# A four-layer vision network on one core: the first convolution and its channel sums, block-diagonal on the full array or as four 64x64 tiles

## What is computed

```python
x = x + _L0_conv_ref(_gn(x), ...)      # shifted-window attention
x = x + _L1_conv_ref(_gn(x), L1_conv_kernel, L1_conv_bias)
x = x + _L2_conv_ref(_gn(x), L2_conv_kernel)
x = x + _L3_conv_ref(_gn(x), ...)      # gated block

def _L1_conv_ref(x, kernel, bias):     # x is the normalised input
    xp = pad(x, one pixel)
    bin_k = sign(kernel)                                  # 3 x 3 x 64 x 64, +1 or -1
    alpha = mean(abs(kernel), axis=(0, 1, 2))
    bin_x = sign(xp)
    beta = mean(abs(xp), axis=3, keepdims=True)
    K = box_sum_3x3(beta) / 9
    return conv3x3(bin_x, bin_k) * (K * alpha) + bias
```

## Time and profile before

| | us |
|---|---|
| median of three runs | 238.65 |
| range of the three | 238.21 to 238.68 |
| profiled execution, its own time | 238.68 |
| its span, first to last instruction | 236.9 |

### The profile page before, as it was taken

How to read it: one execution, slowest core, us unless ns; L and a number is a source line. 1 busy time by engine, 2 the same in 40 slices (tenths; PEclk the granted TensorE clock), 3 DMA queues, 4 the chain that set the end, 5 groups by cost and what they waited for, 6 DMA issues and landing times.

```text
span 236.9 us, 6320 instructions
## 1 busy us (share of the span) xinstructions
PE 217.8 (92%) x2452; PEld 167.4 (71%) x2452; DVE 164.5 (69%) x379; ACT 138.3 (58%) x310; POOL 117.3 (50%) x119
## 2 busy tenths in 40 slices
PE   0668999999999999999999999978799999999995
PEld 0557999999999999999999897444355555434441
DVE  4337697967696968778766874789997865443633
ACT  2146587676767696866786555237654453395651
POOL 5147999995525679754699014837643311010000
PEclk9999999999999999999999999999999999999999
DMA  6997000000000000000000000001126730001012
GB/s 203 235 342 295 3 4 4 0 4 3 0 3 3 3 3 3 3 3 3 0 3 4 0 4 3 0 0 39 42 52 144 163 71 0 1 34 68 34 53 86
DMA packets 5453, 11.34 MB, mean 48 GB/s; under 512 B 816, under 2 KB 4016, under 8 KB 5296
## 3 DMA queue, kind: packets, MB, share of 16 engines
q1 hardware_dynamic: 5280, 10.68, 16.1%
q10 hardware_dynamic: 144, 0.26, 0.3%
HBM read 6.36 MB, written 1.61 MB: 34 GB/s over the span
## 4 chain that ended last, share of the span: by engine, by line
PE 80%; DVE 12%; issue 2%; DMA 2%; POOL 1%; ACT 1%; POOLq 0%; DVEq 0%; ACTq 0%
PE bank L653 18%; PE bank L664 12%; PE bank L681 11%; PE bank L881 5%; PE bank L628 5%; PE bank L882 4%; PE bank L783 4%; PE bank L906 3%; PE bank L896 3%; PE bank L640 3%; DVE x L1112 3%; DVE st L925 2%; PE bank L704 2%; PE bank L768 2%; DMA xw<-xw_in 2%
## 5 line engine op out<-in xcount | busy, mean ns | idle before, releaser
L202 POOL TENSOR_TENSOR kex<-ks,cst 64x784 f32<-64x784 f32 x31 | 47.3, 1525 | 20.7 <-issue 15.3
L986 DVE TENSOR_REDUCE mx<-bank 98x8 f32<-98x392 f32 x64 | 35.7, 558 | 29.0 <-PE bank L653 29.0
L653 PE MATMUL bank<-kex,qbd 128*98 128x196 f32 x256 | 49.4, 335 | 2.0 <-POOL kex L202 2.0
L653 PEld LDWEIGHTS bank<-kex,qbd 128*98 128x98 f32 x256 | 40.3, 167 | 2.9 <-issue 2.2
L991 DVE TENSOR_TENSOR d<-bank,mx 98x392 f32<-98x392 f32 x64 | 36.3, 568 | 2.2
L664 PE MATMUL bank<-cst,d 98*113 98x98 f32 x256 | 33.7, 273 | 1.0 <-DVE d L991 0.9
L284 POOL TENSOR_TENSOR rstd<-ve,mhalf 128x1 f32<-128x1 f32 (+1 forms) x15 | 8.7, 578 | 51.1 <-DVE ve L954 51.0
L455 ACT ACTIVATE pt<-bank 113x392 f32<-113x392 f32 x64 | 28.7, 495 | 6.4 <-PE bank L664 5.6
L664 PEld LDWEIGHTS bank<-cst,d 98*113 98x113 f32 x256 | 28.2, 179 | 3.1 <-DVE d L991 1.3
L681 PEld LDWEIGHTS bank<-vsb,pt 113*49 113x49 f32 x1024 | 26.1, 125 | 5.5 <-issue 4.0
L681 PE MATMUL bank<-vsb,pt 113*49 113x18 f32 x1024 | 29.2, 199 | 0.0
(11 more groups left out here) (103 smaller groups left out, 364.1 us busy)
## 6 DMA issues: line engine op xcount, KB each, us to landing
p<-parts SPq DMA_DIRECT2D x20, 112.5 KB, 2.3
x<-x_in SPq DMA_DIRECT2D x1, 1568.0 KB, 12.6
out<-res SPq DMA_DIRECT2D x8, 196.0 KB, 1.9
xw<-xw_in SPq DMA_DIRECT2D x2, 392.0 KB, 5.2
kex<-kfix_in SPq DMA_DIRECT2D x4, 196.0 KB, 5.9
xw<-xw_in SPq DMA_DIRECT2D x1, 784.0 KB, 9.5
p<-parts SPq DMA_DIRECT2D x6, 108.8 KB, 2.3
qbd<-qfix_in SPq DMA_DIRECT2D x2, 294.0 KB, 7.9
```

The costliest lines, as they stand in the source:

```text
L202: engine.tensor_tensor(kex[q, par, j], ks[q, :].rearrange("p (o t) -> p o t", o=1).broadcast_to([64, 4, RT]), cc("kmask")[q, :].rearrange( ...
L653: mm = pe.matmul(ps_s[s][0:WQ, j * 4 * WT:(j + 1) * 4 * WT], qbd[:, R % NW, j, a], kex[:, R % 2, j, :, a * WT:(a + 1) * WT], start=True, s ...
L986: dve.tensor_reduce(mx[0:WQ, s], sc, AXX, ALU.max).then_inc(max_done, 1)
```

## The change: what it does

`conv1(g)` now handles both halves of a pair of images. For every tap it issues four matmuls of 64x64, one for each quarter of the array: half 0 of the first image on rows 0 to 63 and columns 0 to 63, half 0 of the second on rows 64 to 127 and columns 64 to 127, and half 1 on the two other quarters. So half 1 of the first image arrives on PSUM partitions 64 to 127, and that of the second on 0 to 63. `channel_sums(g)` does the same with the float32 sums, four matmuls for two before. `finish1(g, 1)` puts the images back: two multiplications of 64 partitions each, which read the crossed partitions of the bank and of `ka` and write the straight ones of `prod`. On TensorE both halves of pair 0 stand where the first half did, pair 1 where the second half of pair 0 did, and all of `channel_sums(0)` behind `gather(15)`. On ScalarE `evac_ka(0)` stands behind both `evac_att`.

```diff
--- before.py
+++ after.py
@@ -566,9 +566,9 @@
                         act.wait_ge(z_done, u + 1)
                         act.activation(sz[:, w], bk[2 + w][:, 0:HALF], ACT.Silu).then_inc(sz_ready, 1)
 
-            evac_ka(0)
             evac_att(NR - 2)
             evac_att(NR - 1)
+            evac_ka(0)
             evac_ka(1)
             evac_ka(2)
             evac_ka(3)
@@ -759,16 +759,24 @@
                     pe.wait_ge(x_done, u - 3)
                 return bk[u % 4]
 
-            def conv1(g, i):
-                if i == 0:
-                    pe.wait_ge(sg_ready, g + 1)
-                ps = conv_bank(2 * g + i)
+            def half_of(i, w):
+
+                c = w if i == 0 else 1 - w
+                return slice(64 * c, 64 * c + 64)
+
+            def conv1(g):
+
+                pe.wait_ge(sg_ready, g + 1)
+                ps = [conv_bank(2 * g + i) for i in range(2)]
                 for tap in range(NTAP):
                     ky, kx = tap // 3, tap % 3
-                    mm = pe.matmul(ps[:, 0:HALF], w1[:, tap, :],
-                                   sg1[:, g, ky + i * HR:ky + (i + 1) * HR, kx:kx + HW],
-                                   start=(tap == 0), stop=(tap == NTAP - 1))
-                mm.then_inc(conv_done, 1)
+                    for i in range(2):
+                        for w in range(2):
+                            q = slice(64 * w, 64 * w + 64)
+                            mm = pe.matmul(ps[i][half_of(i, w), 0:HALF], w1[q, tap, q],
+                                           sg1[q, g, ky + i * HR:ky + (i + 1) * HR, kx:kx + HW],
+                                           start=(tap == 0), stop=(tap == NTAP - 1))
+                mm.then_inc(conv_done, 2)
 
             def conv2_stacked(g, i):
 
@@ -811,47 +819,42 @@
                 for i in range(2):
                     conv2_third(g, i)
 
-            def channel_sums(g, i):
-                if i == 0:
-                    pe.wait_ge(box_ready, g + 1)
-                u = 2 * g + i
-                if u >= 2:
-                    pe.wait_ge(ka_ready, u - 1)
-                pe.matmul(bk[5 - i][:, 0:HALF], aw[:], v2[:, g, i * HR:(i + 1) * HR, :],
-                          start=True, stop=True).then_inc(ka_done, 1)
+            def channel_sums(g):
+
+                pe.wait_ge(box_ready, g + 1)
+                if g > 0:
+                    pe.wait_ge(ka_ready, 2 * g)
+                for i in range(2):
+                    for w in range(2):
+                        q = slice(64 * w, 64 * w + 64)
+                        mm = pe.matmul(bk[5 - i][half_of(i, w), 0:HALF], aw[q, q], v2[q, g, i * HR:(i + 1) * HR, :],
+                                       start=True, stop=True)
+                mm.then_inc(ka_done, 2)
 
             turn(LW - 2)
             turn(LW - 1)
             pe.wait_ge(gn_copied, nth(1, NG - 2))
             pe.wait_ge(aw_ready, 1)
-            channel_sums(0, 0)
+            pe.wait_ge(w1_ready, 2)
+            conv1(0)
             gather(NR - 2)
-            pe.wait_ge(w1_ready, 2)
-            conv1(0, 0)
             values(LW - 2)
             values(LW - 1)
             project(NR - 2)
-            conv1(0, 1)
+            conv1(1)
             gather(NR - 1)
-            channel_sums(0, 1)
+            channel_sums(0)
             project(NR - 1)
-            conv1(1, 0)
-            conv1(1, 1)
             mix(col(1, NG - 1), 1, nth(1, NG - 1), ps_qk)
-            channel_sums(1, 0)
-            channel_sums(1, 1)
+            channel_sums(1)
             mix(col(2, 0), 1, nth(2, 0), ps_qk)
-            conv1(2, 0)
-            conv1(2, 1)
-            channel_sums(2, 0)
-            channel_sums(2, 1)
+            conv1(2)
+            channel_sums(2)
             mix(col(2, 1), 1, nth(2, 1), ps_qk)
-            conv1(3, 0)
-            conv1(3, 1)
+            conv1(3)
             pe.wait_ge(w2_ready, 4)
             conv2_stacked(0, 0)
-            channel_sums(3, 0)
-            channel_sums(3, 1)
+            channel_sums(3)
             mix(col(2, 2), 1, nth(2, 2), ps_qk)
             conv2_third(0, 0)
             conv2_stacked(0, 1)
@@ -1107,7 +1110,13 @@
                 xx = xflat[:, g, i * HALF:(i + 1) * HALF]
                 dve.wait_ge(conv_done, u + 1)
                 dve.wait_ge(ka_ready, u + 1)
-                dve.tensor_tensor(prod[:, i], bk[u % 4][:, 0:HALF], ka[:, i], ALU.mult).then_inc(prod_done, 1)
+                if i == 0:
+                    last = dve.tensor_tensor(prod[:, 0], bk[u % 4][:, 0:HALF], ka[:, 0], ALU.mult)
+                else:
+                    for w in range(2):
+                        q, o = slice(64 * w, 64 * w + 64), slice(64 - 64 * w, 128 - 64 * w)
+                        last = dve.tensor_tensor(prod[q, 1], bk[u % 4][o, 0:HALF], ka[o, 1], ALU.mult)
+                last.then_inc(prod_done, 1)
                 dve.wait_ge(prod_done, u + 1)
                 dve.scalar_tensor_tensor(out=xx, in0=prod[:, i], scalar=ww("b1"), in1=xx, op0=ALU.add,
                                          op1=ALU.add).then_inc(x_done, 1)
```

## The result

The changed kernel takes 243.0 us (median of four, 242.72 to 243.51), the kernel before 238.67 beside it: ratio 1.0163, 95% interval 1.0126 to 1.0201. The change makes the kernel slower by 1.6%: 3.9 us by the ratio, 4.3 by the two medians. The profiled execution took 243.51 us, with a span of 241.6.

What follows compares the result with a forecast made beforehand. VectorE was taken to set the time between about 151 and 178 us. A 1.35 us later M plus 1.1 for the lower clock made 2.45 on 238.68, forecasting 241.1 us, range 239.2 to 242.9.

Steps and rivals of the forecast that it cites:

- M: Mark at the start of `mix` for pair 3 of layer two, 155.73 before; predicted 1.35 us later.
- the lower clock behind it: After 6 us of TensorE idling ahead of M, work runs at 1.2 GHz; VectorE's result 1.1 us later relative to M.
- The four tiles run abreast: Tiled convolution: four 64x64 matmuls overlap, so a pair of images takes 1.5 us instead of 3.0.
- A: Trace mark set after measuring: start of the attention's last transpositions (L664), used to compare executions.
- the second fall: Rival: clock low again when the third layer begins, ahead of `channel_sums(3)`; some +3 us, 244, chance 0.06.
- tiles that don't run abreast: Rival: four tiles take 3.0 us per pair of images, M 3.0 later, 242.7 us; chance 0.10.
- E: Mark at the `mix` at 177.97 in the kernel before, behind which nothing is changed.
- The hidden half multiplications: The three other `finish1(g, 1)` cost VectorE 0.50 us each but nothing on the path, covered by GpSimd sums.
- The price of the late first `ka`: First `ka` at 150.47, so the first half's multiplication, formerly done long before, begins at 151.07, on the path.
- Reading PSUM as the limit: Skill's warning that after tiling PSUM reads may limit; by it alone TensorE's gain is worth nothing.
- not slower: Rival: first add starts ahead of GpSimd's sum, M only 0.3 us later, 238.7 us; chance 0.05.

Runs made afterwards that it cites:

- f1: Changed kernel with 30 discarded full-array matmuls between the last projection and the mix of pair 3: 239.96 us, ratio 1.0063.
- a3: The changed kernel measured once more, unedited, for more executions and a second trace: 243.42 us, ratio 1.0184.
- s: Changed kernel with finish1(g, 1) as one multiplication of 128 partitions, second-half images not put back, so output differs: 241.59 us, ratio 1.0116.
- o: Changed kernel with the first channel sum of pair 0 early and its copy ahead of both attention output copies: 241.58 us, ratio 1.0101.
- b2: Run o with the convolution of pair 1 behind project(15) and finish1(0, 0) ahead of residual(14): 241.64 us, ratio 1.0107.
- f2: Run f1 with 12, 10 and 5 more discarded matmuls in the later TensorE gaps: 239.84 us, ratio 1.0036.
- b2f: Run b2 with 12 discarded matmuls ahead of M and the later gaps filled: 238.55 us, ratio 1.0002.
- b5: Run b2f with p2's wait on GpSimd and 8 discarded matmuls instead of 12 ahead of M: 237.00 us, ratio 0.9934.
- p2: Kernel before with GpSimd's second box sum of pair 2 waiting until finish1(0, 1) has added to x: 238.43 us, ratio 0.9965.
- f3: Changed kernel with only the three later gaps filled by discarded matmuls, the gap ahead of M left empty: 242.7 us, ratio 1.0163.

## Why the prediction was right, and where it was not

**The direction and its two mechanisms, the later M and the lower clock behind it, were right.** The four tiles run abreast (starts 3 to 4 ns apart, then 0.17 us), M came 1.47 us later against A for the predicted 1.35, and VectorE read the second `mix` at M + 3.50 (160.06 - 156.56), the predicted M + 3.5. f1, where the read is at M + 1.99, shows that the latter is the clock. At the third `mix` of the stretch, 174.04, the kernel was 17.48 us behind M where it had been 16.38 (172.11): 1.10, the predicted 1.1.

**What failed is the chance of the second fall.** My forecast was 241.1, the result 243.0, just above the range's 242.9 (by the ratio 242.6 to my 238.68, just within it): I forecast 2.4 us of loss and 3.9 came. That this is still about the range is luck. Its top was set for tiles that don't run abreast, which did not happen, and the 244 of the second fall was left out. The rival "the clock falls and is low again when the third layer begins" had 0.06 and +3 us; it happened in both traces, with +2.77 in one and +1.22 in the other. I looked for one long rest, and asked if 2 us of it would be enough. The clock fell at 174.0 after 3.95 us in which TensorE rested 1.93, worked for 0.89 on the channel sums and rested 1.13. In the kernel before the same place has more work between the same waits, since the sums take 1.58 and the rests are 1.51 and 0.44, and no fall. a3 has the same 1.93, 0.89 and 1.13 or 1.14 as the changed kernel's first trace, and the fall. s, o, f1 and b2 have the same 0.89 and 1.13 or 1.14 too, but rest only 1.14 to 1.34 ahead of the sums, because the convolution of pair 3 ran at the lower clock there and took about 3 us; none of them has a fall at this place. Nor has f2, which fills both rests. So the fall came in the two traces with the longest rest and in no other. Whether the rest itself decides, the short work behind it, or how long the clock had been up before, these runs don't separate. With this rival on the path the terms add up: 1.47 + 1.10 + 2.77 = 5.34 us from A to E, and in a3 1.45 + 1.10 + 1.22 = 3.77.

**The hidden half multiplications were hidden**, shown by s against o. **The price of the late first `ka`** was shown by o: 1.43 us, about M's whole delay. s took 0.68 us off the same delay in another way, so the two are not to be added. Reading PSUM as the limit did not come true: in the changed kernel VectorE waited 3.15 us for the first `ka` and then multiplied in 0.57, as before. What limited M in b2f and in the kernel before was GpSimd's hold on the add, as b5 and p2 show. **The rival "not slower"**, GpSimd finding the add ahead of it, is what p2 made to happen in the kernel before, and it is worth 1.44 us up to M.

**What stays open:** why the second fall lasts 3.4 us in one execution and 6.8 in another. And what brings the second fall is only narrowed down, as said above.

## What to carry to other kernels

Work that fills an engine's wait is not free to remove: when TensorE is made faster in a stretch in which it waits for others, read how long and how often it will rest there, and price what comes next at the lower clock. When an operation is moved to make room, ask who was fed by it early; here the late first `ka` cost 1.4 us. And where two engines hold each other up, the order of their starts, a few tenths of a microsecond, may be worth more than the arithmetic: one wait on GpSimd brought M 1.4 us forward.

## What the runs showed of the hardware that was not expected

The two groups of executions, some 2 us apart (238.1 to 239.3 and 240.2 to 241.2 for the kernel before), come from the kernel's start. TensorE in time, run b2, whose A was at 145.33, 2.8 us later than before:

```profile
21.31 2.82 PE L653 MATMUL bank<-kex,qbd 128*98 128x196 f32 x8
```

and the changed kernel:

```profile
19.46 1.49 PE L653 MATMUL bank<-kex,qbd 128*98 128x196 f32 x8
```

The same eight records take 2.82 us in one and 1.49 in the other: by that near doubling TensorE was still at the lower clock in b2 at 21 us, and no longer in the other. The PEclk column reads 1.00 there in both, since the trace has no record of the clock before its first rise; the first record is at 24.4 us in b2 and at 17.0 in the changed kernel. L653 takes 2.82 us in three traces and 1.49 in the ten others. The three of the late kind (b2, p2, f3) have A at 144.5 to 145.3, those of o and b5 at 143.5 and 143.8, all others at 141.9 to 142.7. Since the kernel before has both groups too, a median over few executions can be off by 2 us for a reason that has nothing to do with the edit, which is why the marks were needed.
